# Three orders changed in the loop of a convolution-and-FFN block: GpSimd's normalisation, ScalarE's copies and sums, VectorE's aggregate

## The reference

```python
x = x + _L0_conv_ref(_ln_c(x), fc1_w, fc2_w, sa_w)
t = _to_tokens(x)
t = t + _L0_ffn_ref(_ln_t(t), w1, w2)      # _bitlinear, gelu, _bitlinear; 512 -> 2048 -> 512
# _bitlinear: scale = 127 / max|x| of a token; x_quant = round(x * scale) / scale
```

## Time and profile before

| what | value |
|---|---|
| median of 3 runs | 307.96 us (307.3 to 308.25) |
| the profiled execution | 307.39 us, of which 305.5 us are its span |
| busy: TensorE matmul / VectorE / ScalarE / GpSimd | 266.0 / 232.2 / 230.4 / 160.4 us |
| mean granted TensorE clock | 0.958 of full speed |

### The profile page before, as it was taken

One profiled execution on the slowest core, in us unless ns is written; L12 is line 12 of the kernel. 1 busy time (PEld: TensorE's weight loads), 2 busy tenths in 40 slices (PEclk: granted clock), 3 DMA queues, 4 the chain that ended last, 5 costly groups with the idle time before them and its releaser, 6 DMA issues.

```text
span 305.5 us, 5868 instructions
## 1 busy us (share of the span) xinstructions
PE 266.0 (87%) x1834; PEld 154.6 (51%) x1834; DVE 232.2 (76%) x532; ACT 230.4 (75%) x466; POOL 160.4 (52%) x267
## 2 busy tenths in 40 slices
PE   2557849595999999999999999999999999999973
PEld 2344734482456554655565556555664555444431
DVE  0573769978878898889788978888898887986410
ACT  1873697679588888888888887888788878786821
POOL 8406663515736484549544954494548462467210
PEclk9999965959799999999999999999999999999998
DMA  7999200000345036703770396129512531472483
GB/s 193 379 390 410 75 1 0 2 2 7 62 88 145 11 71 145 200 3 71 168 175 10 63 194 153 29 43 234 112 38 56 150 71 35 89 180 43 69 208 103
DMA packets 71078, 34.20 MB, mean 112 GB/s; under 512 B 52040, under 2 KB 68424, under 8 KB 70536
## 3 DMA queue, kind: packets, MB, share of 16 engines
q1 hardware_dynamic: 69300, 32.78, 42.7%
q10 hardware_dynamic: 1748, 1.05, 1.2%
HBM read 14.94 MB, written 6.29 MB: 70 GB/s over the span
## 4 chain that ended last, share of the span: by engine, by line
PE 53%; DVE 15%; POOL 12%; issue 7%; ACT 5%; DMA 3%; ACTq 2%; SPq 1%; POOLq 0%; DVEq 0%
PE ps_o L1229 18%; PE ps_h L1218 8%; PE ps_t L1218 8%; POOL v L466 5%; PE front L1148 4%; POOL rs L460 3%; DVE st L802 3%; POOL w_room L489 3%; PE small L1164 2%; PE front L1238 2%; DMA taps_rev<-in_L_conv_sa_w 2%; PE front L1138 2%; DVE junk_v L930 2%; PE ps_t L1265 2%; ACT junk_p L551 2%
## 5 line engine op out<-in xcount | busy, mean ns | idle before, releaser
L1229 PE MATMUL ps_o<-w2T,hq 128*128 128x512 f16 x384 | 92.2, 379 | 1.3 <-DMA hq<-w_raw 1.3
L489 POOL TENSOR_SCALAR w_room<-w_room,q 128x1024 f32<-128x1024 f32 x48 | 53.8, 1130 | 31.3 <-DVE q L914 30.1
L904 DVE TENSOR_REDUCE amax<-w_room 128x1 f32<-128x1024 f32 (+1 forms) x48 | 57.9, 1207 | 10.4 <-ACT w_room L551 10.4
L1218 PE MATMUL ps_h<-w1T,xq 128*128 128x512 f16 x208 | 55.2, 405 | 1.8 <-ACT xq L551 1.4
L1229 PEld LDWEIGHTS ps_o<-w2T,hq 128*128 128x128 f16 x384 | 36.6, 98 | 36.6 <-DMA hq<-w_raw 1.8
L551 ACT ACTIVATE w_raw<-w_room 128x1024 f16<-128x1024 f16 x48 | 50.5, 1054 | 0.6 <-POOL w_room L489 0.6
L551 ACT ACTIVATE w_room<-ps_h,s 128x512 f32<-128x512 f32 x52 | 35.8, 689 | 10.5 <-PE ps_h L1218 10.0
L1218 PE MATMUL ps_t<-w1T,xq 128*128 128x512 f16 x176 | 42.6, 379 | 0.0
L551 ACT ACTIVATE w_room<-ps_t,s 128x512 f32<-128x512 f32 x44 | 29.6, 690 | 6.8 <-PE ps_t L1218 6.6
L1218 PEld LDWEIGHTS ps_h<-w1T,xq 128*128 128x128 f16 x208 | 19.7, 104 | 23.7 <-issue 4.3
L551 ACT ACTIVATE junk_m<-front 128x192 bf16<-128x192 f32 x64 | 20.5, 329 | 13.3 <-DVE pooled L815 12.6
(11 more groups left out here) (125 smaller groups left out, 467.1 us busy)
## 6 DMA issues: line engine op xcount, KB each, us to landing
out<-w_room SPq DMA_DIRECT2D x16, 384.0 KB, 3.4
x_in<-in_x SPq DMA_DIRECT2D x14, 384.0 KB, 5.0
w_room<-in_L_ffn_w SPq DMA_DIRECT2D x4, 1024.0 KB, 9.5
w_raw<-in_L_ffn_w SPq DMA_DIRECT2D x4, 1024.0 KB, 12.0
x_in<-in_x ACTq DMA_DIRECT2D x2, 384.0 KB, 4.0
hq<-w_raw SPq DMA_TRANSPOSE x48, 3.1
fc_raw<-in_L_conv_fc_w ACTq DMA_DIRECT2D x2, 128.0 KB, 4.4
taps_rev<-in_L_conv_sa_w SPq DMA_DIRECT2D x1, 0.2 KB
```

The source lines that it names most:

```text
L489: pool.tensor_scalar(part, part, q2[tile.par][:, 0:1], MAGIC, ALU.mult, ALU.add).then_inc(g_rounded, 1)
L904: chain.mark(dve.tensor_reduce(amax2[:, i:i + 1], w1_room[:, first + i * F // 2:first + (i + 1) * F // 2 + i], AX.X, ALU.max, apply_absolu ...
L1218: last = pe.matmul(banks[b], xq[tile.pair.par][:, tile.s, k, :], w1T[:, k, b * 512:(b + 1) * 512], start=(k == 0), stop=(k == NC - 1))
L1229: last = pe.matmul(ps_o[:, :], hq[tile.par][:, k, :], w2T[:, k, :], start=(k == 0), stop=(k == NF - 1))
```

## The change

Four moves, no operation added or removed. On GpSimd, `normalise1(fresh, 2)` goes ahead of the rounding of the first half of the hidden values of tile 1 of the next pair. On VectorE, `aggregate(fresh, 2)`, on which that step waits, goes ahead of `sum_conv` and `add_ffn`, directly behind its `channel_stats`. On ScalarE, `copy_out` goes ahead of the first `pack_g` of tile 1, and `token_mean(att, 1)` and `copy_xq(nxt, 0)` go ahead of the second.

```diff
@@ gpsimd, body
                 if turn:
                     normalise1(fresh, 0, 1)
+                    normalise1(fresh, 2)
                     round_g(Tile(nxt, 1), (0,))
-                    normalise1(fresh, 2)
@@ scalar, body
                 gelu(Tile(pair, 2), blocks=(3,))
-                pack_g(Tile(pair, 1), 0)
                 if pair.c > 0:
                     copy_out(Tile(pair.plus(-1), 2), OUT_BANK[0])
+                pack_g(Tile(pair, 1), 0)
                 if attend:
                     token_mean(att, 0, V1_BANK[0])
+                    token_mean(att, 1, V1_BANK[1])
+                if normalise:
+                    copy_xq(Tile(nxt, 0), XQ_BANK[0])
                 pack_g(Tile(pair, 1), 1)
-                if attend:
-                    token_mean(att, 1, V1_BANK[1])
-                if normalise:
-                    copy_xq(Tile(nxt, 0), XQ_BANK[0])
                 if attend:
                     token_mean(att, 2, V1_BANK[2])
@@ vector, body
                 if turn:
                     channel_stats(fresh, 2)
+                    aggregate(fresh, 2)
                 if attend:
                     sum_conv(att)
                 add_ffn(Tile(pair, 2))
-                if turn:
-                    aggregate(fresh, 2)
```

More of the change, by code:

```diff
@@ L714, in body @@
                 gelu(Tile(pair, 2), blocks=(3,))
-                pack_g(Tile(pair, 1), 0)
                 if pair.c > 0:
                     copy_out(Tile(pair.plus(-1), 2), OUT_BANK[0])
+                pack_g(Tile(pair, 1), 0)
                 if attend:
                     token_mean(att, 0, V1_BANK[0])
-                pack_g(Tile(pair, 1), 1)
-                if attend:
                     token_mean(att, 1, V1_BANK[1])
@@ L724, in body @@
                     copy_xq(Tile(nxt, 0), XQ_BANK[0])
+                pack_g(Tile(pair, 1), 1)
                 if attend:
```

## The result

Over 20 runs of each, the kernel before has a median of 307.53 us (306.82 to 309.04) and the changed one 309.13 us (307.51 to 313.32). The ratio is 1.0042, with a 95% interval of 1.0022 to 1.0062: **slower by 0.4%**, and with a wider spread. The ratio leaves out the one execution of 313.32 us, which counts as a slow run (1.9% above the fastest of its kernel); the other nineteen go up to 311.09. The profiled execution of the changed kernel took 309.48 us, its span is 307.6 against 305.5.

A forecast was written before the change was run, and what follows sets the result against it. TensorE's own work was taken as the bound, only gaps winnable. Turn terms -0.2, +0.27, +0.25 and -0.73 gave -0.41, plus turn 4's 1.14 or 0.09; the middle, about +0.2, gave 308.2 us, range 306.6 to 310.5.

The forecast's parts named there:

- What bounds the kernel: TensorE's own work fills the turn; only three small gaps, 0.73 us a turn in all, can be won.
- copy_out's 0.23: TensorE's gap ahead of turn_v1(att,1), waiting for copy_out to empty its bank; 0.23 us, removed by moving copy_out.
- the third gap: TensorE's gap of 0.19 us between turn_xq(nxt,0) at 176.98 and ffn_in(nxt,0) at 178.59.
- GpSimd and VectorE: aggregate in time, t first, v held 0.35 us, turn_v1's wait gone; turn_xq near 176.4 instead of 176.98.
- VectorE's 0.29: VectorE's token_max, which gates ScalarE's first sum, comes 0.29 us earlier because t starts at 170.87.
- The second packing: On ScalarE, behind token_mean and copy_xq, it starts 0.94 us later, between 0.85 and 1.4.
- The load: load_x of pair+3, last in SP's queue, lands 0.94 us later against 1.05 of room in turns 1 to 4.
- Delta: Further delay of the load from overlap with the next tile's transposing DMA; 0 to 1.4 us, taken as 0.2.
- The end: In turn 7 the second transposing DMA is issued at 289.5 instead of 289.22, stores following: +0.25 us.
- A: Likeliest, 0.42: gaps are won, TensorE gives them back waiting for x; 308.2 us, from 307.1 to 308.9.
- C: Slower, chance 0.34: v reaches SBUF ahead of t, t ends 0.5 us later, packing 1.4 later; 309.5 to 310.5 us.
- its second way: The same price as v ahead of t, reached with t first and a further load delay of 0.65 us.

The follow-up runs named there:

- the mean ahead alone: The changed kernel with minus_mean ahead of the power in normalise1 and nothing else; 308.15 us, ratio 1.0027 to the kernel before.
- the first profile: Profile of the changed kernel in the result's runs, 309.48 us; the second is of the same kernel run again, ratio 1.0097 to the kernel before.

## Why the prediction was right, and where it was off

**What bounds the kernel: right.** TensorE's gaps were all there was to win. turn_v1's wait for GpSimd and copy_out's 0.23 are gone, the third gap too, and the runs with the load first show what that is worth: 0.55 us a turn.

**GpSimd and VectorE: right in kind, off in size.** aggregate was in time, t was first, token_gate was no longer stretched. But I let only v be held, by 0.35; it was the mean, by 0.51, and what stands behind it isn't just GpSimd: `limit` waits for rstd2, 0.39 us. I had counted VectorE's 0.29 as won down to token_max without following limit's second wait. turn_xq won 0.37 instead of 0.54, and ffn_in 0.55 instead of 0.73.

**The second packing: right, 0.23 too small.** Forecast 0.94 later, measured 1.17, at the store 1.26. The 0.29 that I took off is the term that failed: token_max came 0.05 earlier, not 0.29. A second wait was left out: copy_xq, which now stands ahead of the packing, needs turn_xq, and it begins at 177.97 just as turn_xq ends (177.53 plus 0.40). Both come from GpSimd's chain: with the mean ahead alone, turn_xq and the packing are each 0.27 earlier.

**The load: the mechanism and its place were right.** New waits in exactly turns 1 to 4 (0.52, 0.81, 1.01, 0.92 at the matmul in the first profile, 0.36, 0.26, 0.69, 1.39 in the second; forecast 0.6 to 0.9), none in turns 0 and 5. Delta, chosen at 0.2 from bounds of 0 and 1.4, is 0.1 or nothing over all the kernels; in the first profile the loads landed after 5.3 to 5.7, and beyond 5.3 the prediction itself called delta the term at fault. The Trainium skill's ring order (DMA: Bandwidth & Descriptors, Queues, rings and completion order) agrees with the later transposing DMA, which landed 5.2 us after issue in the changed kernel's turn 3 against 3.1 before, in both about 1 us behind the load. A delta of 0, as I read the rule, isn't excluded: the two means lie 0.1 apart.

**The sum.** Forecast a turn: +0.09 in turns 1 to 3; measured +0.13, +0.48, +0.67 (turn_x to turn_x: 29.90, 30.25, 30.44) in the first profile and -0.02, -0.08, +0.38 in the second (29.75, 29.69, 30.15). Turn 4: +1.14 or +0.09 forecast, +0.58 and +1.07 measured. Turn 5: -0.73 forecast, -0.55 measured (28.67 us instead of 29.22). The end: +0.25 forecast, +0.55 measured, of which 0.33 is copy_out's. Turn 0: -0.2 forecast, -0.6 and -0.3 measured from its start to turn_x. In turn 3 of the first profile both terms show: the store is 0.32 later than the forecast's 0.94, and the load takes 0.3 more than 5.0 and delta's 0.2. From the start of turn 0 to the end the two profiles are 1.2 and 1.0 us longer than the one before, where the sum had +0.2. What lies ahead of turn 0 differs by execution (turn 0 starts at 77.7 to 79.5 us in all fourteen profiles), and adds 0.9 to the first profile's span.

The point, 308.2 against a base of 307.96, was +0.1%; measured is +0.42%, inside the range and just beyond the bound of 0.3% up to which I called it no change. That bound divides what I held likeliest (A) from the slower side, and the result lies in A's mechanism with C's sign: C's own mechanism, v ahead of t, didn't occur, but its second way, a delta of 0.65, came near in single turns of the first profile (landings of 5.6 and 5.5 where the kernel before has 5.2 and 5.0). That the time lies inside the range is owed to its width, which takes in C; A's own interval ended at 308.9. The mis-sized terms are the packing's 0.94 (0.23 short, in each of four turns, about 0.9 us in all) and the end's 0.25. I also priced the wait as time lost once; that a long one can lower the clock behind it was not among the rivals.

## What to carry to other kernels

When an instruction is moved ahead of one that feeds a DMA queue, follow the queue past its own DMA to all that stands behind it: here a load with 1 us of room was two entries further, and the change that won 0.55 us a turn was lost through it, and came back whole (0.8 to 1.0% faster) once the load was issued ahead. Gaps in a row on one engine, each closed by another engine, may be won only together: here each half of the change alone won nothing. When two engines disturb each other, follow each instruction's second wait too; here the cheapest fix was to put the small operation first (0.3 us a turn, once the load was out of the way).

## What the runs showed of the hardware that I had not expected

- VectorE's t holds a GpSimd instruction that starts 0.10 us behind it (the mean: 0.70 us for 0.19), but neither is held where GpSimd's started 0.03 us ahead (power 0.55, t 0.75).
- The second of two loads of 384 KB landed 4.9 to 5.6 us after issue behind the stores with no packet of the instruction queues in flight, and 5.7 to 6.7 in eleven of thirteen loads with one. Ahead of the stores it took 3.9 to 4.9 in eighteen of twenty, 5.4 and 5.7 in the others.
- Waits of TensorE of 1.68, 1.82 and 1.91 us were followed by stretches at the lower clock (granted 0.73, 0.50 and 0.75 over 4 us); waits of 1.01, 1.39 and 1.73 us weren't.
